# Query projection of a cross-attention kernel: weight blocks stationary and up to four x tiles moving, with the norm taken by squares summed over partitions

## The reference, cut to what matters

```python
def rms_norm(x, w, eps=EPS):
    y = xf * jax.lax.rsqrt(jnp.mean(xf * xf, axis=-1, keepdims=True) + eps)
    return y.astype(x.dtype) * w
...
q = rms_norm(linear(x, q_w, q_b), norm_q_w).reshape(B, L, NH, HD)
k = rms_norm(linear(ctx_txt, k_w, k_b), norm_k_w).reshape(B, -1, NH, HD)
...
img_x = attention(q, k_img, v_img)
txt_x = attention(q, k, v)
return linear((txt_x + img_x).reshape(B, L, DIM), o_w, o_b)
...
x = x + xattn(_layernorm(x), ctx, ...)
x = x + ffn(_layernorm(x), ...)
```

## Time and profile before

| | us |
|---|---|
| median of 3 runs (1579.1 to 1583.16) | 1582.9 |
| the profiled execution, by its time | 1584.27 |
| its span on the core | 1582.5 |
| PE busy, of the span | 1533.3 (97%) |
| DVE busy | 1186.8 (75%) |
| ACT busy | 712.4 (45%) |
| POOL busy | 702.9 (44%) |
| granted TensorE clock, mean | 0.994 |

### The profile page before, as it was taken

One profiled execution on the slowest core, in us unless ns is written; L12 is line 12 of the kernel. 1 busy time (PEld: TensorE's weight loads), 2 busy tenths in 40 slices (PEclk: granted clock), 3 DMA queues, 4 the chain that ended last, 5 costly groups with the idle time before them and its releaser, 6 DMA issues.

```text
span 1582.5 us, 41314 instructions
## 1 busy us (share of the span) xinstructions
PE 1533.3 (97%) x16262; PEld 1195.2 (76%) x16262; DVE 1186.8 (75%) x1884; ACT 712.4 (45%) x1458; POOL 702.9 (44%) x788
## 2 busy tenths in 40 slices
PE   8999999999999999999999999999997999999997
PEld 6776777777777777777777777777775787777897
DVE  6753788878888788888788887788887586554986
ACT  5763444443444444444434444444444124555441
POOL 6762344344444344443444443444446582114752
PEclk9999999999999999999999999999999999999999
DMA  6843121112211112111122111121114524010000
GB/s 199 247 139 109 59 62 55 49 48 68 72 48 54 48 51 77 60 54 48 48 68 72 48 54 48 54 74 60 54 31 124 189 107 160 28 54 27 1 1 24
DMA packets 66167, 113.70 MB, mean 72 GB/s; under 512 B 21392, under 2 KB 36080, under 8 KB 64576
## 3 DMA queue, kind: packets, MB, share of 16 engines
q1 hardware_dynamic: 65280, 110.20, 22.1%
q0 software_dynamic: 832, 2.75, 0.7%
HBM read 82.59 MB, written 30.34 MB: 71 GB/s over the span
## 4 chain that ended last, share of the span: by engine, by line
PE 88%; ACT 5%; DVE 3%; issue 2%; POOL 1%; DMA 1%; SPq 0%; ACTq 0%; DVEq 0%; POOLq 0%
PE ps L1469 21%; PE ps L1471 19%; PE ps L1470 19%; PE ps L1610 7%; PE ps L1576 6%; PE ps L1551 3%; PE ps L1522 3%; PE ps L1582 2%; PE ps L1823 2%; ACT prob L802 2%; PE ps L1806 2%; PE ps L1815 1%; ACT prob L800 1%; PE ps L1504 1%; PE ps L1586 1%
## 5 line engine op out<-in xcount | busy, mean ns | idle before, releaser
L547 POOL TENSOR_TENSOR prob_img<-prob 128x448 f32<-128x448 f32 x128 | 148.0, 1157 | 216.6 <-ACT prob L802 216.6
L510 POOL TENSOR_TENSOR ctx_lo<-ctx_raw,ctx_hi 128x472 fp32r<-128x472 f32 x64 | 115.5, 1826 | 246.0 <-ACT ctx_hi L743 246.0
L1111 DVE RECIPROCAL rec<-ps 128x224 f32<-128x224 f32 x128 | 199.1, 1556 | 8.8 <-PE ps L1610 3.2
L800 ACT ACTIVATE prob<-ps 119x448 f32<-119x448 f32 x128 | 69.8, 546 | 198.2 <-PE ps L1576 198.2
L1100 DVE TENSOR_REDUCE top<-ps 112x4 f32<-112x1028 f32 x128 | 156.3, 1221 | 0.0
L1105 DVE SCALAR_TENSOR_TENSOR prob_img<-prob,ones_last,prob_img 23x448 f32<-23x448 f32 x128 | 87.5, 684 | 78.2 <-POOL prob_img L547 76.1
L776 ACT ACTIVATE sq_junk<-proj 128x513 bf16<-128x513 f32 (+1 forms) x96 | 61.1, 637 | 172.7 <-DVE proj L1079 172.7
L1099 DVE TENSOR_REDUCE top<-ps 112x4 f32<-112x472 f32 x128 | 83.1, 649 | 65.7 <-PE ps L1551 65.7
L1576 PE MATMUL ps<-q_all,k_all 32*128 32x112 f32 (+1 forms) x3072 | 126.2, 275 | 0.0
L802 ACT ACTIVATE prob<-ps 128x896 f32<-128x896 f32 x128 | 116.9, 913 | 0.0
L1469 PE MATMUL ps<-w_v_img_hi,ctx_hi 128*128 128x512 f32 x256 | 109.9, 429 | 0.0
(11 more groups left out here) (339 smaller groups left out, 4394.9 us busy)
## 6 DMA issues: line engine op xcount, KB each, us to landing
ctx_raw<-in_ctx_dram SPq DMA_DIRECT2D x32, 748.0 KB, 4.2
xh_dram<-xh SPq DMA_DIRECT2D x32, 448.0 KB, 3.1
q_dram<-q_turned SPq DMA_DIRECT2D x28, 256.0 KB, 2.8
q_all<-q_dram SPq DMA_DIRECT2D x32, 224.0 KB, 3.1
out_dram<-out_sb SPq DMA_DIRECT2D x32, 224.0 KB, 2.3
xh<-in_x_dram SPq DMA_DIRECT2D x31, 224.0 KB, 2.8
xa<-in_x_dram SPq DMA_DIRECT2D x21, 256.0 KB, 3.2
ring<-in_wo_dram SPq DMA_DIRECT2D x2, 2048.0 KB, 8.3
```

The lines of the kernel that those rows point to most:

```text
L510: nc.gpsimd.tensor_tensor(ctx_lo[:, :, cols], ctx_raw[:, :, cols], ctx_hi[:, :, cols].bitcast(F32), ALU.subtract).then_inc(ctx_lo_done, 1)
L547: nc.gpsimd.tensor_tensor(prob_img[:, g % 2], prob[:, g % 2, 1, :], prob[:, g % 2, 2, :], ALU.add).then_inc(img_summed, 1)
L800: nc.scalar.activation(prob[0:CHUNK_C, g % 2, 0, :].rearrange("p (j q) -> p j q", j=GH), ps[0:CHUNK_C, 2:6, 0:L], ACT.Exp).then_inc(exp_do ...
L1111: nc.vector.reciprocal(rec[:], bank[:, 2:4]).then_inc(norm_step, 1)
```

## The change

The stationary and the moving operand of the query projection change places. The x tiles come in groups (`GROUPS`): two of 2 tiles, then six of 4. For a group u there are four blocks m of 128 output dimensions. A block is again 12 matmuls, now with a 128x128 block of w_q stationary and the group's 256 or 512 token columns moving, so queries come out with dimensions on partitions, which is the layout that q_dram has; `turn_q` and `q_copy` go. All queues now run over k = 4u + m, 32 steps; x tile t is turned at step k = t for t of 4 and more (at 1 and 3 for tiles 2 and 3), while the group before is projected.

The bias is one value per partition, so ACT adds it as it reads PSUM: `q_keep` writes `q_raw`, `q_squares` writes the squares. The norm is now a sum over partitions: DVE adds the four blocks' squares (`add_squares`, three per group), PE sums over partitions with `ones_col` moving (`sum_squares`, one matmul per tile), ACT adds eps (`q_sums`), POOL takes one power for the group (`inverse_q`, 128x4), PE spreads the inverse over partitions with one transpose per tile (`turn_inverse`) and DVE multiplies (`scale_q`, four per group). SP stores 512 KB at a time, half of a group's blocks.

Three further things move. Of the weight pieces, those with an odd number from 3 on get their lo part on POOL (`piece_rest`) instead of DVE. x tiles are normalised two steps ahead of their turn. At the start PE turns tiles 0 and 1, with 8 more warm-up transposes between them, before any projection, and the projection of group 0 is done in halves of the contraction.

```diff
+GROUPS = [(0, 2), (2, 2)] + [(t, 4) for t in range(4, NT, 4)]
+NU = len(GROUPS)
+TURNED_AT = {1: 2, 3: 3, **{t: t for t in range(4, NT)}}
...
+            def store_q(u, e):
+                two = slice(2 * e, 2 * e + 2)
+                sp.wait_ge(q_scaled, KC * u + 2 * e + 2)
+                sp.wait_ge(q_stored[e], 16 * u)
+                sp.dma_start(q_dram[:, two, group_cols(u)], q_raw[u % 2][:, two, 0:P * GROUPS[u][1]]).then_inc(q_stored[e], 16)
...
-                for k in range(NT + 1):
-                    if k:
-                        inverse_q(k - 1)
-                    if k + 3 < NT:
-                        normalise_x(k + 3)
-                    if k == 23:
+                normalise_x(3)
+                for k in range(KC * NU):
+                    if k % KC == 1 and k > KC:
+                        inverse_q(k // KC - 1)
+                    if k in TURNED_AT and TURNED_AT[k] + 2 < NT:
+                        normalise_x(TURNED_AT[k] + 2)
+                    if k % 2 and 3 <= piece_at(k) < PIECES and piece_at(k) % 2:
+                        piece_rest(piece_at(k))
+                    if k == KC * NU - 2:
...
+            def q_keep(u, m):
+                act.wait_ge(qp_full, KC * u + m + 1)
+                if u >= 2:
+                    act.wait_ge(q_stored[m // 2], 16 * (u - 1))
+                nc.scalar.activation(q_raw[u % 2][:, m, 0:P * GROUPS[u][1]], q_bank(u, m), ACT.Identity, bias=q_bias[:, m:m + 1])
+
+            def q_squares(u, m):
+                if m:
+                    act.wait_ge(q_sq_added, 3 * u + m - 1)
+                else:
+                    act.wait_ge(q_sums_full, u)
+                nc.scalar.activation(q_sq[m > 0][:, 0:P * GROUPS[u][1]], q_bank(u, m), ACT.Square, bias=q_bias[:, m:m + 1]).then_inc(q_sq_done, 1)
...
+            def add_squares(u, m):
+                w = P * GROUPS[u][1]
+                dve.wait_ge(q_sq_done, KC * u + m + 1)
+                if m > 1:
+                    dve.wait_ge(q_sq_added, 3 * u + m - 1)
+                nc.vector.tensor_tensor(q_sq[0][:, 0:w], q_sq[0][:, 0:w], q_sq[1][:, 0:w], ALU.add).then_inc(q_sq_added, 1)
...
+                for k in range(KC * NU):
+                    if k in TURNED_AT:
+                        x_rest(TURNED_AT[k])
+                    if k and (k - 1) % KC:
+                        add_squares((k - 1) // KC, (k - 1) % KC)
+                    if k in TURNED_AT and TURNED_AT[k] + 2 < NT:
+                        ln1(TURNED_AT[k] + 2)
+                    if k % KC >= 2 and k > KC:
+                        scale_q(k // KC - 1, 2 * (k % KC) - 4)
+                        scale_q(k // KC - 1, 2 * (k % KC) - 3)
+                    if k % 2 and piece_at(k) < PIECES and piece_at(k) % 2 == 0:
                         piece(piece_at(k))
...
                 turn_x(0)
-                queries(0, range(0, 1))
+                for _ in range(WARM // 2):
+                    nc.tensor.transpose(ps[:, 5, 0:P], ident[:], ident[:])
                 turn_x(1)
-                queries(0, range(1, 2))
-                for k in range(NT):
-                    if k:
-                        if k + 1 < NT:
-                            turn_x(k + 1)
-                        queries(k)
-                        turn_q(k - 1)
...
+                for m in range(KC):
+                    queries(0, m, range(0, 1))
+                turn_x(2)
+                for m in range(0, 2):
+                    queries(0, m, range(1, 2))
+                turn_x(3)
+                for m in range(2, KC):
+                    queries(0, m, range(1, 2))
+                for k in range(KC, KC * NU):
+                    if k in TURNED_AT:
+                        turn_x(TURNED_AT[k])
+                    if k % KC == 1:
+                        sum_squares(k // KC - 1)
+                    if k % KC == 2:
+                        turn_inverse(k // KC - 1)
+                    queries(k // KC, k % KC)
```

260 lines of the change are left out of this document (149 added, 111 removed).

## The result

The changed kernel took 1588.07 us in the median of 20 runs (1582.54 to 1592.52), the kernel before 1582.15 in 20 runs beside it (1577.87 to 1583.72): 1.0038 of the time, with a 95% interval of 1.0029 to 1.0047, or 5.9 us slower. The forecast was 1585, +2, in a range of 1576 to 1592; the time lies in the range, in the class "slower by over 0.3%" that had a chance of 0.25. A later comparison of the same two kernels gave less, 1583.87 against 1580.84, 1.0016 [1.0006, 1.0026], 2.5 us by the ratio.

The account below looks back on a forecast made before the run. PE was taken to bound the query prologue. Keys +0.2, last group's norm +0.85 and x loads +0.5 gave +1.6, rounded to +2 on a 1582.9 median: 1585 us (chance 0.48), range 1576 to 1592.

Parts of the forecast that it names:

- 0.5 at step 10: Query projection, once groups have four tiles: 0.5 us of waiting added to the time when queries end.
- three times 1.1: Full-width steps where POOL's weight piece meets DVE's add_squares: PE waits 1.1 us at each of three, 3.3 in all.
- the x path's pace: Normalising, turning and rounding x tiles: 5.7 us per two steps, 6.75 with a hold; too slow for 256-column steps at 4.1.
- block 8: First query block with 512 columns: forecast to start at 36.9 us, with 24 tiles left to project.
- the start: First projection: PE needs tiles 0 and 1 first, so it starts at 12.4 us, 2.6 later than before.
- rival (c): Clock in group 0 stays slow: 48 matmuls cost 0.085 us more each, +4, half in waits, 1587 us; chance 0.07.
- the forecast's 0.2: End of the queries: first key matmul at 123.7 us against 123.49 before, +0.2.
- The tail: Behind the first key matmul: last group's sum_squares and turn_inverse replace the last turn_q, 1.2 us for 0.35, +0.85.
- rival (b): DVE and SP become the bound, x loads behind stores landing after over 4.0 us: +7, 1592 us; chance 0.20.
- (a): x path keeps up in the small groups and no holds follow: keys start at 117.0, 1577 us; chance 0.20.
- (d): All of PE's saving is had, about 9 us less the start's 2.6 and tail: 1576 or below; chance 0.05.
- within 0.3%: Whole-kernel class "same", 1578.2 to 1587.6 us, as a measurement can tell about 0.3%, 4.7 us; chance 0.53.

Follow-up runs that it names:

- the changed kernel with the edit in the hidden layer: Changed kernel with ACT instead of DVE adding the 1.0 to the MLP hidden layer's exponential: 1583.10 us, 1.0009 of the kernel before.
- the edited pair: Kernel before and changed kernel, both with ACT instead of DVE adding the hidden layer's 1.0: 1579.51 and 1583.10 us, 3.6 us apart.

## Why the prediction was partly right

**Bound and work.** Right that PE bounds the steady groups and that its waits there are few: 3.1 us measured against 3.8 taken (0.5 at step 10 and three times 1.1). Right that matmuls of 256 columns go by their columns, 0.12 us apart (0.128 taken), and not by the 0.19 of a weight load; and that the groups of two run at the x path's pace.

**Mis-sized: sum_squares.** Taken 0.40 a group, measured 0.81. The step that failed is the reading of the earlier trace rows: the x8 there are records, and I took them for matmuls. Of the six sums from block 8 on five have four tiles and make 2.05 us more on PE (the first has two tiles, and took the forecast's 0.4); by the run with doubled sums such work counts in full only in the two groups without an odd piece, and lies in waits for POOL in the others. A count of records has to be divided by what one instruction of the source makes of them.

**Mis-sized: the start.** Block 8 was to start at 36.9 and did at 39.31. The chain of queues was right where the clock came early: in the changed kernel with the edit in the hidden layer turn_x(2) to (8) are at 15.07, 18.25, 22.34, 24.67, 30.16, 33.52 and 36.08, against 15.5, 18.9, 22.3, 25.6, 31.0, 33.8 and 36.4. Some of that is luck, since its granted clock was 0.50 for most of the time from 31 to 35 us, which the forecast did not have. What I gave 0.07 as rival (c), that group 0 stays at the lower level, happened in six of nine profiles without extra filler, and it costs 2.7 to 3 us up to turn_x(2), not 4 with half in waits. The argument "eight transposes may bring it sooner, but PE idles" stopped short of a chance. The rows of before had the lower level at 12.1 us and the upper at 14.8, behind one wait of 1.84; here two waits, 1.01 and 1.41, lie between 9.7 and 13.2, and the upper level came at 17.4. One execution was no ground for the 0.07.

**From block 8 to the keys.** Forecast 86.8 us, measured 88.7. Of the 1.9 between them, the sums add 2.05; the waits, taken 0.7 too high, and the first inverse, of two tiles and so 0.25 shorter, take 0.95 away. The 0.8 that is left has no place; waits read too short from modelled ends would fit it, which is not shown. So the +4.5 at the keys is the forecast's 0.2, 2.4 from the start and 1.9 from here. Of an execution with the clock early, like the edited changed kernel's (124.43), the forecast of 123.7 was 0.7 short.

**The holds.** Their size came out and their way did not, so the size was luck. I took 1.1 for each odd piece, by POOL holding DVE's addition or the reverse. The trace of the changed kernel shows DVE first and both a little longer (0.3 and 0.4), and what PE waits for is POOL's power and x behind the piece. With the squares in PSUM 2.6 us of the groups go: the term is real, with the holds spread over the groups and not on three steps. The Trainium skill (SBUF — State Buffer, SBUF: two separate sides) has the engine that starts first block the other for the whole instruction; the one-column addition that took 2.29 us agrees, and the hidden layer, where DVE stood through the rest of one instruction of POOL and three more, goes beyond it. There are 24 such additions in the kernel; the prediction's 21 is a miscount.

**Tail and loads.** The tail was right: 0.85 taken, 0.8 measured. That the code behind the prologue is the same was taken to mean the same time, a term put at nothing; it is 1.2 us over the batches. From 40 us on the loads of x tiles land after 5.0 us in the median (3.0 to 6.7, of 17 issues; all 28 have 3.5, against 3.2 in the earlier trace rows), so the condition of rival (b), over 4.0, was met, and its consequence did not come: DVE waited for them 1.1 us in two places. Issuing loads first brought the keys 0.8 sooner.

**The rivals.** (a) and (d) fell, since the x path does hold the groups of two. So did (b), and the range had its two ends from (a) and (b): that the time lies in it is owed to its width more than to the sum, which was 4.3 us short at the keys in that profile. The chance of 0.53 on "within 0.3%" fits the second comparison and the edited pair better than the first; the first put it just beyond.

## What to carry to other kernels

An edit of a few microseconds is read at the last instruction that it touches, in several profiles, and not from the two totals: a hold of 4.7 us and several places where the clock may fall lie between there and the end. When an elementwise step is added on DVE beside a busy POOL, try it with one operand in PSUM: here, at the same width, it neither held nor was held, and cutting its width to one column did nothing against the hold.
